# Adding expert rows to the output in memory, instead of storing them and adding them up in a last stage

## The reference

```python
edge_index = jnp.stack([src, dst])
x = x + gnn(_layernorm(x), edge_index, edge_weight, W_l, b_l, W_r, b_r, att, bias)   # attention over the edges, 8 heads of 32
x = x + ffn(_layernorm(x)[None], Wg, bg, W1, b1, W2, b2)[0]

# ffn: 8 experts, hidden size 512, every node goes to the 2 experts with the highest gate scores
gate_scores = x @ Wg + bg
_, idx = jax.lax.top_k(gate_scores, 2)
mask = jax.nn.one_hot(idx, 8).sum(axis=-2)
h = gelu(einsum('td,edh->teh', xf, W1) + b1)
y = einsum('teh,ehd->ted', h, W2) + b2
out = einsum('ted,te->td', y, mask)
```

## Time and profile before

| | |
|---|---|
| median of 3 runs | 1939.84 us (1938.97 to 1940.76) |
| span of the profiled execution, which is its own time | 1942.8 us |
| TensorE busy | 1707.9 us, 88% |
| VectorE busy | 1467.7 us, 76% |
| ScalarE busy | 1247.9 us, 64% |
| GpSimd busy | 1213.6 us, 62% |
| data moved | 372.87 MB, 192 GB/s over the span |
| mean granted clock of TensorE | 0.937 |

### The profile page before, as it was taken

The page is one execution under the profiler, slowest core; times in us unless marked ns, Lnnn a source line. Parts: engine busy times, 40 slices in busy tenths (PEclk is TensorE's granted clock), DMA queues, the critical chain, the costliest instruction groups (busy, mean ns, idle before and its releaser), DMA issues. The chain is left out here.

```text
span 1942.8 us, 35858 instructions
## 1 busy us (share of the span) xinstructions
PE 1707.9 (88%) x9397; PEld 1450.3 (75%) x9398; DVE 1467.7 (76%) x2732; ACT 1247.9 (64%) x3160; POOL 1213.6 (62%) x1338
## 2 busy tenths in 40 slices
PE   4785689999999999999999999994977999999950
PEld 3664578878887887888878787873967999999940
DVE  6683689989999999999999999997884334333425
ACT  2353479989999999999999999884711333333310
POOL 3675777777777777777777777732455555555510
PEclk9897899999999999999999999998578999999975
DMA  6678777878778787878777778743802222222229
GB/s 227 158 230 262 215 241 236 244 225 240 238 241 240 237 242 237 239 245 242 236 239 241 237 245 240 237 133 121 300 20 71 71 70 70 70 70 70 70 90 333
DMA packets 217937, 372.87 MB, mean 192 GB/s; under 512 B 45061, under 2 KB 103661, under 8 KB 217597
## 3 DMA queue, kind: packets, MB, share of 16 engines
q1 hardware_dynamic: 157217, 214.44, 33.6%
q0 software_dynamic: 52992, 147.92, 27.1%
q10 hardware_dynamic: 7564, 8.65, 1.3%
HBM read 316.77 MB, written 55.32 MB: 192 GB/s over the span
## 5 line engine op out<-in xcount | busy, mean ns | idle before, releaser
L798 POOL DMA_INDIRECT rows<-left_rows,idx x880 | 841.9, 957 | 272.4 <-issue 267.9
L1128 PE MATMUL p_row<-rights,hotT 128*128 128x256 f32 x1760 | 503.9, 368 | 54.5 <-issue 27.5
L1130 PE MATMUL p_row<-rows,ident 128*128 128x256 f32 x1760 | 529.9, 383 | 0.0
L1191 PE MATMUL p_gain<-W,hots 128*128 128x264 f32 x1760 | 473.6, 393 | 9.3 <-DVE acc L983 7.5
L1128 PEld LDWEIGHTS p_row<-rights,hotT 128*128 128x128 f32 x1760 | 322.1, 192 | 130.4 <-issue 81.4
L1191 PEld LDWEIGHTS p_gain<-W,hots 128*128 128x128 f32 x1760 | 324.3, 190 | 83.3 <-issue 20.5
L1018 ACT ACTIVATE L<-p_row 128x512 f32<-128x512 f32 x440 | 259.4, 590 | 129.3 <-PE p_row L1130 126.9
L954 DVE TENSOR_TENSOR W<-rows,p_weights 128x1024 f32<-128x1024 f32 x220 | 267.0, 1214 | 48.5 <-PE p_gain L1191 45.8
L1088 ACT ACTIVATE far<-iota_row,dl 128x128 f32<-128x128 f32 x880 | 299.2, 391 | 0.0
L1617 ACT ACTIVATE e_hT<-e_ph,b_column 128x128 f32<-128x128 f32 x420 | 120.0, 368 | 267.3 <-PE e_ph L1642 267.3
L863 DVE TENSOR_TENSOR L<-L,p_weights 128x1024 f32<-128x1024 f32 x220 | 266.1, 1210 | 27.8 <-ACT L L1018 27.8
(11 more groups left out here) (244 smaller groups left out, 1918.1 us busy)
## 6 DMA issues: line engine op xcount, KB each, us to landing
rights<-right_rows SPq DMA_DIRECT2D x440, 256.0 KB
locals<-item_locals SPq DMA_DIRECT2D x110, 256.0 KB, 3.8
rows<-left_rows,idx POOLq DMA_INDIRECT x880
right_rows<-p_parts SPq DMA_DIRECT2D x49, 256.0 KB
c_rows<-results SPq DMA_DIRECT2D x12, 1024.0 KB, 13.5
w<-in_L_ffn_W SPq DMA_DIRECT2D x16, 512.0 KB, 6.5
left_rows<-p_y SPq DMA_DIRECT2D x49, 132.0 KB
kept_rows<-X SPq DMA_DIRECT2D x7, 896.0 KB, 4.8
```

The lines of the kernel that those rows point to most:

```text
L798: nc.gpsimd.indirect_dma_start(out=rows[:, g.slot(RINGS), n, :], out_offset=None, in_=d["left"][:, :], in_offset=bass.IndirectOffsetOnAxis ...
L1128: nc.tensor.matmul(to, hotT[:, g.slot(2), i, :], rights[:, g.slot(2), n, part * D:(part + 1) * D], start=(part == 0), stop=False)
L1130: last = nc.tensor.matmul(to, s["ident"][:, :], rows[:, g.slot(RINGS), i, 0:D], start=False, stop=True)
L1191: last = nc.tensor.matmul(p_gain[:, n, 0:D + H], hots[:, g.slot(2), i, :], W[:, g.slot(2), i, :, :].rearrange("p h c -> p (h c)"), start=( ...
```

## The change

The output in memory gets 6400 rows, of which the first 6250 are returned. `route` stores the residual rows there: after the seven stores of normed rows, SyncE issues seven stores of X and one more, of the last tile again, into the 128 rows behind the last tile (rows 6272 to 6399); it waits for all of them at its end. The scatters of `experts` write to `out` with an addition done by the DMA. A node's two rows now go to the same place, so the two choices no longer need two values, and two VectorE instructions of the tables go. Slots without a node all go to the 128 rows behind the last tile, each lane to its own. Since an addition reads its destination and writes it later, each scatter waits for the one before it to have landed. `results` and `combine` are gone.

```diff
-NOWHERE = 2 * NT * P
+NOWHERE = NODE_TILES * P
...
-            results=dram("results", (NOWHERE + SLOT_TILES * P, D)),
+            out=out,
...
-        combine(nc, d, s, out)
...
-        value = sb("r_value", [P, RT, 2])
+        value = sb("r_value", [P, RT])
...
-                nc.gpsimd.iota(value[:, :, :], [[P, RT], [NT * P, 2]], base=P, channel_multiplier=1,
+                nc.gpsimd.iota(value[:, :], [[P, RT]], base=P, channel_multiplier=1,
...
-                nc.gpsimd.iota(nowhere[:, :], [[P, SLOT_TILES]], base=NOWHERE + P, channel_multiplier=1,
+                nc.gpsimd.iota(nowhere[:, :], [[0, SLOT_TILES]], base=NOWHERE + P, channel_multiplier=1,
...
+                for b in range(BATCHES):
+                    sp.dma_start(d["out"][b * BY * P:(b + 1) * BY * P, :].rearrange("(t p) f -> p t f", p=P),
+                                 X[:, tiles_of(b), :]).then_inc(residual_kept, 16)
+                sp.dma_start(d["out"][NOWHERE:NOWHERE + P, :], X[:, last_tile, :]).then_inc(residual_kept, 16)
                 sp.wait_ge(kept, 16 * BATCHES)
+                sp.wait_ge(residual_kept, 16 * (BATCHES + 1))
...
-                                                value[:, t, k:k + 1], ALU.is_equal, ALU.mult)
+                                                value[:, t:t + 1], ALU.is_equal, ALU.mult)
...
-                step(nc.vector.tensor_scalar(spare_f[:, :], got, float(P + NT * P), -float(NT * P), ALU.is_ge, ALU.mult))
-                step(nc.vector.scalar_tensor_tensor(token_f[:, :], got, -float(P), spare_f[:, :], ALU.add, ALU.add))
-                step(nc.vector.tensor_scalar(s["comes_from"][:, :], token_f[:, :], 0.0, None, ALU.max))
+                step(nc.vector.tensor_scalar(s["comes_from"][:, :], got, -float(P), 0.0, ALU.add, ALU.max))
...
                 def send(t):
                     pool.wait_ge(done, t + 1)
+                    if t > 0:
+                        pool.wait_ge(stored[(t - 1) % 4], 16 * ((t - 1) // 4 + 1))
                     nc.gpsimd.indirect_dma_start(
-                        out=d["results"][:, :], out_offset=bass.IndirectOffsetOnAxis(ap=s["goes_to"][:, t:t + 1], axis=0),
-                        in_=y[:, t % 4, :], in_offset=None).then_inc(stored[t % 4], 16)
+                        out=d["out"][:, :], out_offset=bass.IndirectOffsetOnAxis(ap=s["goes_to"][:, t:t + 1], axis=0),
+                        in_=y[:, t % 4, :], in_offset=None, compute_op=ALU.add).then_inc(stored[t % 4], 16)
...
-def combine(nc, d, s, out):
...
-    args.append(nc.dram_tensor("out", (N, D), F32, kind="ExternalOutput").ap())
+    args.append(nc.dram_tensor("out", (NT * P, D), F32, kind="ExternalOutput").ap())
     build(nc, *args)
-    return run_bass_kernel_spmd(nc, [arrays], core_ids=[0]).results[0]["out"]
+    return run_bass_kernel_spmd(nc, [arrays], core_ids=[0]).results[0]["out"][0:N]
```

More of the change, by code:

```diff
@@ L1212, in route @@
     w_in = s["w_in"] = sem("w_in_experts")
+    residual_kept = sem("r_residual_kept")
     with ExitStack() as scope:
@@ L1229, in route @@
         nowhere = sb("r_nowhere", [P, SLOT_TILES])
-        token_f, spare_f = sb("r_token_f", [P, SLOT_TILES]), sb("r_spare_f", [P, SLOT_TILES])
+        spare_f = sb("r_spare_f", [P, SLOT_TILES])
         before, every = sb("r_before", [P, P]), sb("r_every", [P, P])
```

## The result

The changed kernel takes 1980.92 us (median of 4 runs, 1978.08 to 1983.19) against 1940.3 us for the kernel before: ratio 1.0206, 95% interval 1.0193 to 1.0218. It is 2.1% slower. I had forecast 1883 us. The profiled execution has a span of 1976.4 us, against 1942.8 us. That execution took 1978.08 us, the fastest of the four, so its span is 1.7 us short of its own time; I had taken the two for the same. The profiled execution of the kernel before, whose own time is not on record, is a long one: its span is longer than all four times measured, 1938.97 to 1942.27 us. That is why the spans differ by 33.6 us and the medians by 40.6.

What follows compares the result with a forecast made beforehand. Expert stage set by TensorE, then a gap and a transfer-bound tail; 1942.8 - 58.6 (tail) - 0.55 (route) + 2.55 (last scatters) = 1886.2 us of span, less 3.0: 1883 us. Forecast's own range 1879 to 1888 us, whole range 1878 to 1983.

Steps and rivals of the forecast that it cites:

- The last stage: Transfer-bound tail after the expert stage, from 1884.2 us to the span's end at 1942.8 us: removed, 58.6 us less.
- The end of the block: Time from the last scatter's landing to the next stage's first instruction, 9.6 us, kept whole in the changed kernel.
- The route: Stage before the first gather: fewer VectorE steps save 0.55 us; added residual stores hide behind VectorE's row maps, costing 0.
- The rule for the wait: Expert stage: waiting for the scatter before is free while L + 0.28 us is at most the stage's 3.72 us period.
- The size of the period: One GpSimd cycle per scatter in the expert stage, priced at 3.48 us, 0.24 us below 3.72, so hidden.
- L: Landing time of an accumulating scatter, from issue to reported completion: priced at 3.2 us, between bounds 2.4 and 5.2.
- the start: Step on GpSimd from a semaphore to the next scatter's issue, priced at 0.28 us.
- The fixed part is paid once: Within a scatter's landing, making and reporting the transfer stays 1.8 us; the add brings only 0.8 us of reading.
- Rival A: GpSimd's scatter instruction grows by 0.49 us with addresses per row: period 3.97 us, median 1909 us; chance 0.20.
- break-even: Scatter period at which the waits use up the removed tail's gain: 4.27 us, with a landing of 3.99 us.
- Rival B: GpSimd's chain of landing and issue bounds the expert stage: 1983 us at a landing of 4.4 us; chance 0.28.
- From span to time: Step from profiled span to median time: median taken 3.0 us below the span, 1886.2 us to 1883 us.

Runs made afterwards that it cites:

- e1: Changed kernel with the wait for the scatter before kept and the addition left out: 2363.22 us on a slower chip, ratio 0.9786 to the kernel before.
- e6: Changed kernel, scatters after tile 7 waiting only at an expert's first tile, 15 spare blocks for slots without a node, everything computed: 1882.09 us, ratio 0.9700.
- e10: Changed kernel with half of each row's bytes in the scatters and the landing's wait carried by the scatter's own instruction: 1882.89 us, ratio 0.9696.
- e3: Kernel before with additions in its scatters, no wait between them, and results filled with rows of X first: 2435.53 us on a slower chip, ratio 1.0069.
- e8: Changed kernel with only the first 64 rows of each tile in the scatters: 1910.15 us, ratio 0.9843 to the kernel before.
- e9: Changed kernel with its two waits swapped, so the scatter's own instruction carries the landing's wait: 1927.07 us, ratio 0.9925 to the kernel before.
- e7: Changed kernel with only the first 128 columns of each row in the scatters: 1926.91 us, ratio 0.9933 to the kernel before.
- e2: Changed kernel with its two waits swapped, the scatter carrying the landing's wait, on a slower chip: 2400.73 us, ratio 0.9929 to the kernel before.

## Why the prediction was wrong, step by step

**The last stage, 58.6 us: right.** It is gone, and e1 (56 us), e6 (59 us) and e10 (58 us) show the gain whenever the expert stage keeps its pace. The end of the block, which I kept at 9.6 us, took 6.0: 3.6 us better than priced.

**The route: right.** From its first load to the first gather the kernel before needs 129.15 us (1341.26 to 1470.41), the changed one 128.59 (1336.38 to 1464.97): 0.56 us less, priced at 0.55. The first load of the kernel before is this row:

```profile
1341.26 0.39 SPq L1305 DMA_DIRECT2D X<-kept_rows  x1
```

The residual stores are hidden, and faster than I had bounded them (213 to 386 GB/s, where I took 191 and 131).

**The rule for the wait: right.** Free up to a period of 3.72 us: e1 and e10, which wait before every scatter with landing and start together below it, lie at 3.73 and 3.74 us per tile, like e3 and e6, where the chain is gone. TensorE is busy for all of the windows shown of e3, e6 and e10.

**The size of the period: this is the step that failed.** I priced L at 3.2 us and the start at 0.28, together 3.48 and "hidden"; on the mean the chip took 3.86 and 0.81, together 4.67, which is over 3.72, so the chain set the pace. Both terms were mis-sized, L by 0.66 us and the start by 0.53. The landing has two parts. The data phase I had nearly right: 0.6 + 0.8 = 1.4 us priced, 1.3 measured. "The fixed part is paid once" was wrong: I took 1.8 us for it, and it measured 2.5 (3.8 - 1.3). The growth lies ahead of the data: from the scatter's start to its data it is 1.5 us before (1825.87 to 1827.4) and 2.2 us now (1825.95 to 1828.1), and the instruction itself grew by as much, 0.99 to 1.59 us. Rival A had named that growth (0.49 us) at a chance of 0.20, for the wrong reason: it argued by addresses per row, and e8 shows that halving the rows takes away only 0.16 us. The start is the miss that no rival held: I read 0.28 us from a scatter that carried its only wait, and moved it over to one with two, where the one that comes last stands in an instruction of its own. e9 prices that at 0.51 us per tile. Either miss alone would have broken "hidden", and left the change faster all the same: e9, with the priced start and the long landing, has a ratio of 0.9925 and 4.16 us per tile, and e7, with a landing of 3.3 us and the late start, 0.9933 and 4.17 us, both below the break-even of 4.27.

**The landing, compared.** The high figure of the Trainium skill for HBM's access latency ("DMA: Bandwidth & Descriptors", Latency and other measured facts), 2 us at high load, did give 4.4 us for L, an estimate of mine, and so a time near the measured one; the trace doesn't bear the mechanism out, since gathers in the same stage still land after 2.8 us. The Trainium skill ("Collectives: The Full Stack", The bandwidth ceiling) puts the halved rate of a reduce-scatter between cores down to a transfer of two reads for one write. The rate in the data phase halved here too, 219 to 101 GB/s; but the time for which the 16 DMA engines are busy in it went from 0.6 x 0.63 = 0.38 to 1.3 x 0.92 = 1.20 us, three times as much, and the packets changed from four rows to one, so no run here shows that the second read is the cause.

**Rival B** is what happened, GpSimd's chain as the bound: a chance of 0.28, break-even at 4.27 us, its time at a period of 4.68 us 1983 us; measured were 4.67 us and 1980.92 us. That it had the period is luck: its landing of 4.4 us was some 0.5 us too long and its start of 0.28 us as much too short.

**From span to time.** I let the median lie 3.0 us below the profiled span, as it did before. For the changed kernel it lies 4.5 us above. These 7.5 us are spread between executions and no part of the mechanism; the other 90.2 us of the miss (1976.4 - 1886.2) are in the span.

## What to carry to other kernels

A wait that makes single transfers into a chain has to be priced as the whole cycle, landing and the start of the next issue, against the period of the engine that bounds the stage; where only a quarter of a microsecond is left and one of the terms has never been measured, that is no cover. On GpSimd, look which wait the DMA instruction itself carries: the one that comes last belongs there. And before accepting a chain, ask where two transfers can really meet: here at the 7 tiles where the expert changes, out of 105, and waiting there (and still at tiles 1 to 7) turned 2% slower into 3% faster.

## What the runs showed of the hardware that I had not expected

- An indirect DMA of 128 rows of 1 KB with an addition keeps GpSimd 1.59 us (plain: 0.99) and lands after 3.8 us (plain: 2.4), in 128 packets of one row (plain: 32 of four rows). Of 64 rows it still takes 1.43 us, of rows half as long 1.59 us.
- Its 128 KB keep the 16 DMA engines 92% busy for 1.3 us; with half the bytes 0.7 us at 98%.
- A scatter starts about half a microsecond later after the landing it waits for when that wait is a separate instruction in front of it (0.81 us on the mean) than when it carries the wait itself (0.28 us in e9, 0.27 us in e2).
